# A down-weight schedule moved: other steps for the weight butterflies, the bank users and the low halves of a fused two-layer kernel

## The reference

```
# layer 0, attention: 32 heads of 16, 8 KV heads
q, k, v = x @ Wq, x @ Wk, x @ Wv
a = softmax(q k^T / 4) v ;  y = a @ Wo
# layer 0, feed-forward (on its normalised input), gated into the residual
x = fwht(x * SU_ug) / 64
h = silu(x @ W_gate.T * s_gate) * (x @ W_up.T * s_up)       # 2048 wide
x = fwht(h * SU_dp) / 64
x = x @ W_down.T * (Wscale_dp * 64)
```

## Time and profile before

| | |
|---|---|
| median of 3 runs | 1330.53 us (1328.27 to 1334.45) |
| the profiled execution | 1330.53 us, of which the span of the instructions is 1328.7 us |
| PE busy | 1239.3 us (93%) |
| DVE busy | 1055.6 us (79%) |
| ACT busy | 784.2 us (59%) |
| POOL busy | 542.1 us (41%) |
| mean granted TensorE clock | 0.994 of full |

### The profile page before, as it was taken

How to read it: one execution, slowest core, us unless ns; L and a number is a source line. 1 busy time by engine, 2 the same in 40 slices (tenths; PEclk the granted TensorE clock), 3 DMA queues, 4 the chain that set the end, 5 groups by cost and what they waited for, 6 DMA issues and landing times. The chain is left out here.

```text
span 1328.7 us, 23536 instructions
## 1 busy us (share of the span) xinstructions
PE 1239.3 (93%) x8738; PEld 639.5 (48%) x8738; DVE 1055.6 (79%) x1825; ACT 784.2 (59%) x1306; POOL 542.1 (41%) x464
## 2 busy tenths in 40 slices
PE   4787899999999999999799999999999999999998
PEld 2332333334333433333345548655585546855475
DVE  6788988788888888899768877697696985878856
ACT  4775777678867887688277533465234652365432
POOL 3599863223212321233034734166232762238431
PEclk9999999999999999999899999999999999999999
DMA  6665755896789768877970221102401023002121
GB/s 228 231 153 101 110 94 93 153 161 130 127 154 158 141 120 147 164 143 127 235 288 24 61 47 51 41 8 62 96 10 40 24 50 85 18 33 56 35 35 48
DMA packets 344337, 135.59 MB, mean 102 GB/s; under 512 B 312256, under 2 KB 331424, under 8 KB 341920
## 3 DMA queue, kind: packets, MB, share of 16 engines
q1 hardware_dynamic: 329760, 126.22, 44.7%
q0 software_dynamic: 2048, 6.29, 1.8%
q10 hardware_dynamic: 12416, 1.57, 1.1%
HBM read 44.87 MB, written 17.87 MB: 47 GB/s over the span
## 5 line engine op out<-in xcount | busy, mean ns | idle before, releaser
L1189 PE MATMUL bank<-rows,both 128*128 128x512 f16 x1024 | 237.5, 382 | 6.1 <-DVE both L644 2.6
L965 ACT ACTIVATE probs<-vpair,top_n 128x512 f16<-128x512 f32 x256 | 170.2, 687 | 117.7 <-DVE top_n L655 116.9
L655 DVE TENSOR_REDUCE top_n<-vpair 128x1 f32<-128x512 f32 x256 | 170.1, 684 | 66.7 <-PE bank L1158 66.6
L1203 PE MATMUL bank<-dn,h 128*128 128x512 f16 x768 | 180.5, 382 | 0.0
L965 ACT ACTIVATE probs<-bank,top_n 128x512 f16<-128x512 f32 x256 | 164.3, 687 | 0.0
L655 DVE TENSOR_REDUCE top_n<-bank 128x1 f32<-128x512 f32 x256 | 163.7, 681 | 0.0
L1189 PEld LDWEIGHTS bank<-rows,both 128*128 128x128 f16 x1024 | 94.8, 98 | 129.0 <-issue 16.6
L458 POOL TENSOR_TENSOR h<-th,h 128x512 f16<-128x512 f32 x59 | 68.3, 1157 | 150.4 <-ACT h L934 150.0
L2270 PE MATMUL bank<-rows,both 128*128 128x512 f16 x512 | 117.2, 379 | 0.0
L1203 PEld LDWEIGHTS bank<-dn,h 128*128 128x128 f16 x768 | 71.1, 98 | 92.0 <-issue 15.9
L2286 PE MATMUL bank<-both,hid 128*128 128x512 f16 x512 | 111.2, 379 | 0.0
(11 more groups left out here) (359 smaller groups left out, 2568.6 us busy)
## 6 DMA issues: line engine op xcount, KB each, us to landing
h<-in_ug SPq DMA_DIRECT2D x8, 1024.0 KB, 7.2
lt_scratch<-big SPq DMA_DIRECT2D x16, 384.0 KB, 3.0
dn<-in_down SPq DMA_DIRECT2D x2, 2048.0 KB, 11.7
x_scratch<-th POOLq DMA_DIRECT2D x16, 256.0 KB, 4.9
res<-x_scratch SPq DMA_DIRECT2D x16, 256.0 KB, 4.1
out_x<-res SPq DMA_DIRECT2D x16, 256.0 KB, 2.0
both<-in_w SPq DMA_DIRECT2D x4, 774.0 KB, 6.6
t_scratch<-tok SPq DMA_DIRECT2D x16, 192.0 KB, 2.1
```

What stands on the lines that cost most here:

```text
L655: v.tensor_reduce(top_n[:, i:i + 1], SC_[n % G][:, :], AX.X, ALU.max, negate=True).then_inc(S["max_done"], 1)
L965: a.activation(probs[:, k % TAKEN, j * T:(j + 1) * T], SC_[j][:, :], ACT.Exp, bias=top_n[:, i:i + 1]).then_inc(S["p_ready"], 1)
L1189: mm = pe.matmul(GB[n % 2][:, :], w[:, kt, col:col + P], xnb(b, kt), start=r == 0, stop=r == 2 * KT - 1)
L1203: mm = pe.matmul(bk, h16(ft, r // 2)[:, rows], dn16(ft, r % 2), start=j == 0 and r == 0, stop=j == FT - 1 and r == 2)
```

## The change

It alters three constants and the place of two calls in DVE's loop.

```diff
-DN_AT = (50, 51, 52, 55, 56, 57, 58, 59, 60, 63, 64, 65, 66, 67, 68, 69)
-DN_PAIR_AT = (22,) + tuple(range(25, 48)) + tuple(range(48, 64, 2))
+DN_AT = (49, 51, 52, 53, 55, 57, 58, 59, 60, 61, 62, 63, 65, 66, 67, 68)
+DN_PAIR_AT = (16, 18, 19, 22, 23) + tuple(range(25, 41)) + tuple(range(41, 62, 2))
-LOW_FIRST = 5
+LOW_FIRST = 3
                 p, r = divmod(t - PREP, 4)
+                if t % 2 and t - 1 in DN_AT:
+                    low_down(DN_AT.index(t - 1))
                 if r == 2 and 0 <= p < NCH:
                     take_sum(p)
...
                     row_max(G * (ta // 2))
                 if b < B and m > FFN_STEP and m % 2:
                     gate_mul(b, (m - FFN_STEP) // 2)
-                if t % 2 and t - 1 in DN_AT:
-                    low_down(DN_AT.index(t - 1))
                 if paired:
                     for j in range(1, G):
                         row_max(G * (ta // 2) + j)
                 if t % 2 and 0 <= (t - 3 - FFN_STEP) // 2 < LOW_FIRST:
                     low_rows((t - 3 - FFN_STEP) // 2)
+                if b < B and m > FFN_STEP and m % 2:
+                    up_mul(b, (m - FFN_STEP) // 2)
                 if t % 2 and t in DN_AT:
                     low_down(DN_AT.index(t))
-                if b < B and m > FFN_STEP and m % 2:
-                    up_mul(b, (m - FFN_STEP) // 2)
```

## The result

The changed kernel takes 1339.89 us (median, 1338.0 to 1343.46), the kernel before 1330.53 us: 1.0075 of before, 95% interval 1.0053 to 1.0097, so slower by 0.75%. Forecast were 1338.7 us and slower. Timed once more on another chip the ratio was 1.0075 again (1.0059 to 1.0092). The profiled execution of the changed kernel lies above its median, 1343.82 us with a span of 1342.0 us.

A forecast was written before the change was run, and what follows sets the result against it. POOL's full queue (70 to 157 us) and then a nearly always busy PE (steps 49 to 71) were taken as the bounds; 3.2 + 5.0 = 8.2 us on 1330.53 us gave 1338.7 us, range 1331 to 1343 us.

The forecast's parts named there:

- Part 1: Step 24: earlier pairs make POOL's chunk late; PE waits 3.6 us more, 1.7 us gets through, swallowed by Part 2.
- Part 2: Steps 41 to 43: low row of tile 3 on POOL behind 22 pairs makes up_mul 3.2 us late.
- Part 3: Low half first in DVE's order: gains 0.58 us in step 59, 0.6 us in 51, 1.56 us in 69.
- Part 4: Odd tile's low half last, done 5.9 us after the scores: PE waits 1.0 us in step 60.
- Part 5: Steps 53 and 61: down tile and projection both use MISC; PE idles 2.2 us ahead of each projection.
- The sum of steps 49 to 71: Pairs of steps added up: 71.2 us against 66.2 us before, 5.0 us more, bounds 2 to 7 us.
- I carry a delay of step 71 to the end in full: Behind step 71 the same chain continues and layer 1 starts when layer 0 ends, so none is made good.
- Rival 4: Clock falls too, at steps 43, 53 or 61, some 1.6 us; one or two falls give 1340.3 to 1342 us; chance 0.16.
- Only the bank: POOL is ready in time and only the bank in steps 49 to 71 costs; 1335.5 us; chance 0.12.
- only POOL: Only the POOL wait counts and the bank comes out even; 1333.7 us; chance 0.12.
- Not slower: Low half first decides, today's waits go and the late row is absorbed; 1327 us; chance 0.08.

The follow-up runs named there:

- repeat: The changed kernel again with no edit, for a second profile; 1341.86 us against 1332.69 us for the kernel before, ratio 1.0075.
- experiment 1: POOL's half of the change alone (new pair steps and LOW_FIRST = 3) on the kernel before; 1334.12 us, ratio 1.0012.
- experiment 2: The new steps of the pairs alone on the kernel before, LOW_FIRST still 5; ratio 1.0026.
- experiment 4: POOL's half of the change, but the five early pairs behind their chunks in steps 20 and 24, against the kernel before; ratio 1.0043.
- experiment 8: Of the new DVE order only the front place (even tile's low half first), on the kernel before; ratio 1.0002.
- experiment 6: The new steps of the down tiles alone on the kernel before, DVE order and POOL as before; ratio 1.0027.
- experiments 7: The new DVE order alone (both moved calls) on the kernel before, tiles in their old steps; ratio 1.0019.
- experiment 5: The bank's half alone (new tile steps and new DVE order) on the kernel before, POOL as before; ratio 1.0038.
- experiment 3: LOW_FIRST = 3 alone on the kernel before, pairs where they were; ratio 1.0007.

## Why the prediction came out right, step by step

**Part 1, the pairs ahead of the chunk: mechanism right, size wrong.** The chunk began where it was forecast (93.1 us, late start taken off) and its wait grew from 0.73 to 4.55 us (3.8 us; forecast 3.6). The step that failed is "what gets through to it is some 1.7 us". What got through was 3.15 us by the scores of step 31. Two things were left out. The clock fell behind this wait in all four profiles that have the early pairs: after, its repeat, and experiments 1 and 2. I had listed steps 43, 53 and 61 as places for that and not this, the longest of the new gaps. And DVE's L595 ended with POOL's instruction each time, so that a DVE 3.1 us late (after, experiment 2) and one 3.6 to 3.7 us late (repeat, experiment 1) came out 3.15 us late alike. How much of the 3.15 us is the clock and how much the late POOL is not shown: no run has the wait without the fall. By step 41 it is 3.9 us, most of the rest because the low row of tile 0 took 1.30 us on DVE, beside POOL, in place of 0.68.

**Part 2, the low row behind 22 pairs: the wait that ended last, as forecast.** In the changed kernel POOL starts the row at 157.11 us and `up_mul` of tile 4 follows at 158.40 us. With the late start of 2.55 us taken off these are 154.56 and 155.85 us, forecast 154.7 and 155.95. That is 3.1 us behind the 152.75 us of before, and it is what the 3.0 us of the first stretch consist of. So the agreement is no accident. Wrong was that the DVE work saved gives nothing. By part 1 alone `up_mul` of tile 4 came 3.9 us late (experiment 2). Without the low row of tile 3 ahead of it (1.49 us on DVE before) DVE was ready 2.3 us late, and the 0.77 us of waiting for POOL make it 3.1. In experiment 4, which takes the chunk's wait away, the same `up_mul` waits 3.32 us and comes 3.8 us late, 2.0 of which it owed to steps ahead. Either cause is enough for the whole delay, and they do not add: without the early pairs' place 3.7 us, without the low rows 3.9 us, with both 3.05 us. Undoing either one alone would have gained nothing.

**Part 3, the low half first:** the odd tile's wait went, but experiment 8 shows 0.6 us of loss for the place by itself. My 0.58 and 0.6 us were no gain, because the even tile waited instead. The gain in step 69 did come (4.54 us for the pair of steps, 6.81 before), but from the tile steps: experiment 6 has it with the old order (4.35 us).

**Part 4, the low half last:** 1.12 us ahead of step 60 (forecast 1.0). In experiments 7 and 8 it is the costlier of the two moves, 2.1 us.

**Part 5, two users in a step:** 2.30 us each (forecast 2.2).

**The sum of steps 49 to 71:** 70.38 us in the repeat, against 71.2 forecast. The eleven pairs, forecast and measured: 5.9 / 5.63, 6.05 / 5.94, 8.6 / 8.63, 5.05 / 5.12, 6.55 / 6.26, 7.05 / 6.99, 9.65 / 9.50, 5.9 / 5.97, 5.6 / 5.61, 6.2 / 6.18, 4.7 / 4.54. The sum is 0.8 us too high, most of it in pairs 49 and 57 (0.3 us each). In pair 57 the term mis-sized is the tile behind weighing: I took its start at 2.80 us and its slot at 0.97 us from the earlier trace rows, and measured are 2.62 us (as 187.24 against 184.62 in step 53) and 0.86 us. The two halves do not simply add: tile steps alone 2.0 us, order alone 2.7 us, together 4.1 us.

**From 7.1 to 9.4 us.** Up to step 71 the traces give 3.0 + 4.1 = 7.1 us with the clock full in the second stretch. The measured medians differ by 9.4 us here and 9.2 us on the other chip, with intervals from 7.1 and from 7.9 us upward. The step that failed is "I carry a delay of step 71 to the end in full": the wait of step 89 for a DMA, with the fall of the clock behind it, adds 3.15 and 3.94 us, and 1.1 and 1.0 us come back at layer 1. The sum had no term for it. So the forecast of 8.2 us is 1.1 us too high for the changed steps, and that it lies so near to the 9.4 us is luck. Why the DMA is late there stays open, since no experiment touches it. No profile with one half of the change alone waits in step 89 (four of the others wait 0.3 to 1.0 us for the same DMA in step 97), and the timed halves, 1.0012 and 1.0038, leave 0.25% or 3.3 us to the whole, which is about its size; their intervals are nearly as wide. Rival 4 is in the number too. The first profile has one more fall, in step 61, and experiment 5 one in step 53, each of 1.55 to 1.7 us. The mean granted clock of the timed runs of the repeat is 0.9862 against 0.9882 before, which with PE busy nearly throughout is some 2.5 us; this is worked out from means of a few runs, and it includes the falls of steps 24 and 89.

**The rivals.** Only the bank (experiment 5: 1.0038) and only POOL (experiment 1: 1.0012) each fall short of 1.0075, and either half alone lengthens its own stretch in the trace: both halves cost. Not slower failed where it said it would: the low half of step 53 ended 5.9 us after the scores and not by 3.8.

## What to carry to other kernels

Work put earlier into an in-order queue that is already full does not come earlier; it makes what stands behind it late. Look for the next thing with a deadline behind it, and then for what has one further on, since experiment 3 paid nothing at the first moved row and 2.09 us at the third.

A single bank with an eviction in two stages (ACT, then DVE) must be reckoned from the scores of the step: which instructions stand ahead of the second stage in its queue. When two delays in a row meet the same chain, they do not add, and a trace of the sum shows of the second only what the first left over (0.77 us here); a run with the first removed shows it whole (3.32 us).

A comparison of traces must be followed to the end of the program. The changed steps end at step 71, and some third of the difference arose in step 89, in a transfer that the change does not mention.

## What was not expected of the hardware

A wait of 4.55 us was followed by two float32 matmuls of 1.91 us in place of 1.02. Waits of 2.30 us brought the clock down in step 61 of one of two profiles of the same kernel and in step 53 of another kernel, at 1.55 to 1.7 us each; the steps 49 to 71 otherwise repeat to 0.02 us. A DVE instruction on 8 elements a partition with two SBUF inputs took 0.35 to 0.96 us, depending on when the POOL instruction beside it ended. Also, the scores of step 23 stand between 89.29 and 93.71 us in the profiles of this study, though nothing changed stands ahead of them in PE's queue; one profile's span is no measure of a change of 0.5%.
